# Biased maxima in two halves of the heads, first key units beside the last feed-forward chunks, gated products on GpSimd

## The reference

```
q, k, v = x Wq', x Wk', x Wv'   (32 heads of 8);   q, k = rope(q), rope(k)
gate[h, s, n] = q[h, s] . mean of k over chunk n (32 keys); later chunks out, own chunk always in; best 4 chunks chosen
p = softmax over the keys s' <= s in a chosen chunk of (q . k) / sqrt(8);   o = p v
o = o * rsqrt(mean(o^2) + 1e-6) * o_norm_weight * sigmoid(x Wg1' Wg2');   x1 = layernorm(x + o Wo')
u -> u + shared experts(u) + sum over 4 of 16 routed experts of gating * relu(u w1 + b1) w2 (+ biases);   out = layernorm(x1 + that)
```

## Time and profile before

| | us |
|---|---|
| median of 3 runs | 1453.25 (1452.52 to 1456.14) |
| the profiled execution | 1453.75 |
| its span in the trace | 1451.7 |
| maxima, one turn with feed-forward: first to last reduction | 54.3 |
| last reduction to first exponential | 10.9 |
| first to last exponential | 37.8 (38.6 and 38.7 in turns 1 and 3) |
| turn 0: the same three | 48.2, 8.9, 38.2 |
| busy share of the span | PE 92%, DVE 75%, ACT 58%, POOL 37% |

### The profile page before, as it was taken

The page is one execution under the profiler, slowest core; times in us unless marked ns, Lnnn a source line. Parts: engine busy times, 40 slices in busy tenths (PEclk is TensorE's granted clock), DMA queues, the critical chain, the costliest instruction groups (busy, mean ns, idle before and its releaser), DMA issues.

```text
span 1451.7 us, 29057 instructions
## 1 busy us (share of the span) xinstructions
PE 1332.4 (92%) x10992; PEld 738.7 (51%) x10992; DVE 1087.7 (75%) x2747; ACT 842.7 (58%) x1266; POOL 533.9 (37%) x638
## 2 busy tenths in 40 slices
PE   5677999999998999999999999989999899999597
PEld 3422475535754366534755356543665347553364
DVE  6994688957897578966889578975889668885434
ACT  5406774396735876277743967358762877439121
POOL 3203542254323642245422553235432454225143
PEclk8667999999999999999999999999999999999799
DMA  6001022200321021210222003210112102220031
GB/s 243 16 15 17 16 79 76 52 17 16 104 66 38 30 59 60 74 31 16 82 71 55 16 17 102 71 33 30 60 62 71 31 16 68 73 53 23 13 113 58
DMA packets 52283, 77.81 MB, mean 54 GB/s; under 512 B 6334, under 2 KB 26800, under 8 KB 51888
## 3 DMA queue, kind: packets, MB, share of 16 engines
q1 hardware_dynamic: 52144, 75.96, 18.0%
HBM read 67.02 MB, written 8.65 MB: 52 GB/s over the span
## 4 chain that ended last, share of the span: by engine, by line
PE 61%; DVE 19%; ACT 11%; DVEq 3%; issue 3%; DMA 2%; POOL 1%; SPq 0%; POOLq 0%
PE PS L562 14%; PE PS L574 13%; PE PS L718 8%; ACT UQ L992 7%; PE PS L492 7%; PE PS L509 3%; DVE hr L1163 3%; ACT UK L992 2%; DVE CM L1356 2%; DVEq L1155 2%; PE PS L773 2%; PE PS L413 2%; DVE CM L1275 2%; PE PS L728 2%; PE PS L483 2%
## 5 line engine op out<-in xcount | busy, mean ns | idle before, releaser
L1051 POOL TENSOR_TENSOR hp<-hr,hp 128x512 f16<-128x512 f32 (+1 forms) x200 | 237.1, 1186 | 584.1 <-ACT hp L849 520.0
L1356 DVE TENSOR_REDUCE CM<-PS 128x32 f32<-128x1024 f32 x320 | 376.2, 1218 | 23.2 <-PE PS L492 18.9
L574 PE MATMUL PS<-W,hp 128*128 128x256 f16 (+1 forms) x2400 | 323.2, 274 | 4.6 <-POOL hp L1051 3.6
L562 PE MATMUL PS<-x1T,W 128*128 128x512 f16 (+1 forms) x1200 | 320.6, 385 | 0.0
L840 ACT ACTIVATE hr<-PS,CF 128x512 f32<-128x512 f32 (+1 forms) x200 | 137.2, 686 | 234.3 <-PE PS L562 234.3
L574 PEld LDWEIGHTS PS<-W,hp 128*128 128x128 f16 (+1 forms) x2400 | 216.9, 98 | 96.1 <-issue 34.7
L849 ACT ACTIVATE hp<-hr 128x512 f16<-128x512 f32 (+1 forms) x178 | 112.5, 632 | 169.3 <-DVE hr L1163 156.2
L1163 DVE TENSOR_TENSOR hr<-hr,gB 128x512 f32<-128x512 f32 x176 | 126.2, 717 | 64.9 <-ACT hr L840 58.5
L992 ACT ACTIVATE UK<-PS 128x1024 f32<-128x1024 f32 x160 | 153.0, 1037 | 11.4 <-PE PS L509 11.0
L562 PEld LDWEIGHTS PS<-x1T,W 128*128 128x128 f16 (+1 forms) x1200 | 107.7, 100 | 100.7 <-issue 34.9
L992 ACT ACTIVATE UQ<-PS 128x1024 f32<-128x1024 f32 x160 | 150.9, 1041 | 3.1 <-PE PS L509 1.4
(11 more groups left out here) (150 smaller groups left out, 1793.8 us busy)
## 6 DMA issues: line engine op xcount, KB each, us to landing
gB<-gates SPq DMA_DIRECT2D x64, 256.0 KB, 3.3
gB<-gates SPq DMA_DIRECT2D x32, 224.0 KB, 2.9
gB<-gates SPq DMA_DIRECT2D x32, 192.0 KB, 2.9
gB<-gates SPq DMA_DIRECT2D x32, 160.0 KB, 2.6
xT<-in_xT SPq DMA_DIRECT2D x8, 512.0 KB, 5.8
qET<-rows SPq DMA_DIRECT2D x16, 256.0 KB, 5.2
v<-in_x SPq DMA_DIRECT2D x8, 512.0 KB, 4.1
gB<-gates SPq DMA_DIRECT2D x32, 128.0 KB, 2.9
```

What stands on the lines that cost most here:

```text
L562: mm = pe.matmul(PS[0:w, BK_H[c % 2], :], W1[:, a, k, bass.ds(f0, w)], x1T[:, e, k, :], start=(n == 0), stop=(n == 5))
L574: mm = pe.matmul(PS[:, BK_Y + j // 2, (j % 2) * D:(j % 2 + 1) * D], hp[0:w, slot, a, j * P:(j + 1) * P], W2[0:w, e, bass.ds(c, 1), :].rear ...
L1051: nc.gpsimd.tensor_tensor(hp[0:w, slot, 1, :], hr[0:w, slot, :], hp[0:w, slot, 0, :], ALU.subtract).then_inc(pool_hp, 1)
L1356: nc.vector.tensor_reduce(dst, src, AX.X, ALU.max).then_inc(dve_cm, 1)
```

## The change

The arithmetic stays the same. What changes is where the work stands:

- The biased maxima are made in two halves of 16 heads. The first half stands on the DVE among the reductions, after those of units 20 to 23 (`maxima(j, 0)`); the second after the last reduction. `negT` becomes [16, 2, 512], its first half copied by ACT, its second by the DVE.
- The rows of `qET` go in two sets, `s_rows[0]` for heads 0 to 15, sent while the maxima of the others go on (SP, ahead of the gates of chunk 24), and `s_rows[1]`. The first key units wait for `s_rows[0]` alone; unit 20 waits for `s_rows[1]`.
- `C_MAX` is (11, 23) in place of (11, 22) and `DEALT` has 88 parts for the 40 units in place of 77. The output gate and the transposes of the first half stand among them, in the bank that the next chunk will use.
- What is left of chunks 22 to 24 (one up, eleven down parts) and the transposes of the second half stand between the key units of groups 0 and 1.
- The gated products of chunks 11 to 22 move from the DVE to POOL, ahead of `low`. Those of 23 and 24 stay on the DVE with `split=True`, and so does the relu of chunk 24.
- The first ten key units use two pairs of banks and not three.

```diff
-PAIRS = ((0, 1, 0, 1, 0), (2, 1, 0, 2, 1), (0, 1, 2, 0, 1), (2, 0, 1, 2, 1))
-BACK = ((2, 2, 2, 2, 2), (3, 3, 3, 3, 3), (3, 2, 4, 3, 3), (3, 3, 3, 3, 2))
+PAIRS = [n % 2 if n < 2 * NU else (2, 0, 1)[(n - 2 * NU) % 3] for n in range(TU)]
+BACK = [next((k for k in range(1, n + 1) if PAIRS[n - k] == PAIRS[n]), 0) for n in range(TU)]
-C_FIRST, C_TOPK, C_MAX, C_BIAS = (0, 3), (3, 11), (11, 22), (22, 25)
+C_FIRST, C_TOPK, C_MAX, C_LATE = (0, 3), (3, 11), (11, 23), (23, 25)
-for _c in range(1, MC):
+for _c in range(1, MC + 1):
     DEALT += [(_c, 0), (_c - 2, 4), (_c, 1), (_c - 2, 5), (_c, 2), (_c - 2, 6), (_c - 1, 3)]
-DEALT += [(MC - 2, 4), (MC - 2, 5), (MC - 2, 6)]
+AT_SEL, AT_GATE, AT_NEG = (1, 2), (3, 4), 8
+HALF = H // 2
...
# SP
+                    if m < B - 1 and c == NC - 1:
+                        bias_rows(m + 1, 0)
...
# PE, among the maxima
+                        if part == 2 and cc in AT_GATE:
+                            gate_half(c, AT_GATE.index(cc))
+                        if part == 2 and cc == AT_NEG:
...
+                            maxima_rows(BK_H[(c + 1) % 2], 0)
...
# PE, key units and outputs
+                    if n < RING:
+                        pe.wait_ge(dve_cm, (b + 1) * TU + n + 1)
+                    if n == 2 * NU and m is not None:
                         pe.wait_ge(dve_z, 2 * m + 3)
+                    if n == TU // 2:
+                        pe.wait_ge(s_rows[1], 64 * (b + 1))
...
+                pe.wait_ge(s_rows[0], 64 * (b + 1))
+                unit(0, 0)
+                unit(0, 1)
+                late_up(NC - 1, (0, 1))
+                unit(0, 2)
+                late_up(NC - 1, (2,))
+                late_down(NC - 3, (1,))
+                unit(0, 3)
+                late_down(NC - 3, (2, 3))
+                unit(0, 4)
+                late_down(NC - 2, (0, 1))
+                unit(1, 0)
+                late_down(NC - 2, (2, 3))
+                unit(1, 1)
+                if m is not None:
+                    pe.wait_ge(s_hid, m * NC + NC + 1)
+                maxima_rows(BK_H[1], 1)
+                unit(1, 2)
+                if m is not None:
+                    pe.wait_ge(s_hid, (m + 1) * NC + 2)
+                outputs(0, 0, 0)
+                unit(1, 3)
+                late_down(NC - 1, (0, 1))
+                outputs(0, 0, 1)
+                unit(1, 4)
+                late_down(NC - 1, (2, 3))
+                outputs(0, 0, 2)
+                outputs(0, 0, 3)
...
# POOL
+                    for c in range(*C_MAX):
+                        gated(m, c, c % 2)
+                        low(m, c, c % 2)
+                    for c in range(*C_LATE):
                         low(m, c, c % 2)
...
# DVE, among the reductions and after them
+                        if TU // 2 <= u < TU // 2 + NT:
+                            maxima(u - TU // 2, 0)
+                if m is not None:
+                    gated(m, NC - 2, (NC - 2) % 2, split=True)
                 for j in range(NT):
...
+                    maxima(j, 1)
+                if m is not None:
+                    dve.wait_ge(pe_h, m * NC + NC)
+                    dve.wait_ge(pool_hp, m * NC + NC)
+                    s_last = (NC - 1) % 2
+                    nc.vector.tensor_scalar(hr[:, s_last, :], PS[:, BK_H[s_last], :], b1[:, NC - 1:NC], 0.0, ALU.add,
+                                            ALU.max).then_inc(s_hid, 1)
+                    dve.drain()
+                    gated(m, NC - 1, s_last, split=True)
+                dve.wait_ge(pe_neg, 2 * b + 2)
+                nc.vector.tensor_scalar(negT[:, 1, :], PS[0:HALF, BK_H[1], :], 1.0 / UNIT, None, ALU.mult).then_inc(dve_neg, 1)
```

More of the change, by code:

```diff
@@ L257, in build @@
         act_neg = sem("act_neg")
-        s_rows = sem("s_rows")
+        dve_neg = sem("dve_neg")
+        s_rows = [sem(f"s_rows{n}") for n in range(2)]
         pe_g1 = sem("pe_g1")
@@ L644, in selection_rows, with gate_half, maxima_rows @@
                     mm.then_inc(pe_sel, 1)
+                def gate_half(c, i):
+                    if m is not None:
+                        pe.wait_ge(s_hid, m * NC + c + 2)
+                    r = ROW_G1 * i
+                    for j in range(2):
+                        mm = pe.matmul(PS[:, BK_H[(c + 1) % 2], j * D:(j + 1) * D], g1T[r:r + HD, j * P:(j + 1) * P],
+                                       WG2[r:r + HD, :], start=True, stop=True, tile_position=(r, 0))
+                    mm.then_inc(pe_g, 1)
+                def maxima_rows(bank, n):
+                    pe.wait_ge(dve_bias, (2 * b + n + 1) * NT)
+                    for j in range(NT):
+                        mm = pe.transpose(PS[0:HALF, bank, j * P:(j + 1) * P], negm[:, j, HALF * n:HALF * (n + 1)], ident)
+                    mm.then_inc(pe_neg, 1)
                 if m is None:
@@ L668, in late_up, with late_down @@
+                def late_up(c, parts):
+                    for part in parts if m is not None else ():
                         up(m, c, part)
-                def late_down(c):
-                    for j in range(NT):
+                def late_down(c, parts):
+                    for j in parts if m is not None else ():
                         down(m, c, c % 2, j)
-                if m is not None:
-                    late_up(NC - 3)
-                    late_up(NC - 2)
-                    late_down(NC - 4)
@@ L942, in turn @@
                             high(m, c, (C_TOPK[0] + u) % 2)
-                for i in range(0, MAX_STEPS):
-                    for u in range(MC):
-                        c = i * MC + C_MAX[0] + u
-                        if m is not None:
-                            relu(m, c, (C_MAX[0] + u) % 2)
-                        if i == 0 and u in (1, 2):
-                            act.wait_ge(pe_sel, 2 * b + u)
-                            nc.scalar.activation(stage_sel[u - 1], PSH[:, BK_H[(c + 1) % 2], :].rearrange("p (q s) -> p q s", q=2),
-                                                 ACT.Copy, scale=-OFF).then_inc(act_sel, 1)
-                        if m is not None:
-                            high(m, c, (C_MAX[0] + u) % 2)
@@ L1132, in _ @@
         def _(dve):
[L1133 removed]
+            for credit in (dve_x1, dve_z, dve_o, dve_otok, s_gated):
                 dve.sem_inc(credit, 1)
```

197 lines of the change are left out of this document (89 added, 108 removed).

## The result

| | before | after |
|---|---|---|
| median of 4 runs, side by side | 1454.70 us (1452.52 to 1456.21) | 1520.59 us (1518.06 to 1523.06) |
| ratio | | 1.0454 (95% interval 1.0425 to 1.0483) |
| span of the profiled execution, granted clock | 1451.7 us, 0.961 | 1521.0 us, 0.941 |
| first to last reduction, turns 1 to 7 | 54.3 | 62.3 (turn 7: 65.1) |
| last reduction to first exponential | 10.8 to 11.9 | 0.3 |

The kernel became 66 us slower; 33 were forecast. The direction and the places are the forecast ones, the size is twice it. Seven turns at +9.95 us (69.6), -1.4 in turn 0 and +1.1 in all the rest are the 69.3 us by which the spans differ.

The account below looks back on a forecast made before the run. PE bounds the maxima, a DVE-to-DMA chain ends the tail, ACT's exponentials run back to back. Seven turns at +6.4 - 1.4 = +5.0 us (+35.0) and turn 0 at -1.8 give +33.2: 1453.25 + 33.2 = 1486 us, range 1450 to 1505.

Parts of the forecast that it names:

- The maxima: First to last reduction: PE's added parts, gates and transposes, with waits, lengthen it by net 6.4 us a turn.
- it falls some 2 us behind with a ring of two, which I price at 0.4 us of PE: Maxima, units 20 to 23: the DVE's new work exceeds its slack; the lag costs PE 0.4 us a turn.
- The 3.25 us of the half: DVE time for one half, 16 heads, of the biased maxima, put at 3.25 us; the whole block took 4.50.
- The upper bound of 7.5: Maxima stretch: largest growth a turn, 7.5 us, with the DVE's lag paid in full; lower bound 5.3.
- From the last unit to exponential 13: Last max unit's start to group 2's fourth exponential: 25.4 us before, 24.0 after, a gain of 1.4 a turn.
- the strict order: Behind the last max unit, masks, outputs, finish and uncovered norm follow in sequence; copy_outputs(0) ends at 22.0 us.
- The clock: Rival: idle PE at to_tokens(0) drops to 1.2 GHz; five more turns at 0.9 us, 4.5 us, 1491; chance 0.10.
- POOL's product: Gated product moved to POOL: 1.19 us each, its chain of 4.0 us hidden in a chunk's round of 4.8.
- its rival of 1520: POOL's product costs 2.37 us, so PE waits 0.4 us for each of twelve chunks: 1520; chance 0.05.
- The faster rival's point: Start kept, 1418, if copy_outputs(0) ends by 14.3 us after the last unit's start; 22 counted; chance 0.15.
- Turn 0: Turn without feed-forward: maxima +7.6 us, gap before the first exponential -9.4, together -1.8.
- the signs of being right: Maxima 60 us, start within 0.5, exponentials 47, ACT waiting some 8, copy without idle before it, PE waiting over 4.

Follow-up runs that it names:

- a_nomask: Changed kernel with the masked sum of the first half of the biased maxima left out (bias not computed there): 1508.71 us, ratio 1.0380 to the kernel before.
- a_warm: Changed kernel with 10 and 18 filler matmuls, results unused, in PE's two waits among the exponentials: 1500.73 us, ratio 1.0319 to the kernel before.
- a_copy: Changed kernel with copy_outputs(0) ahead of the layer norm in the DVE's finish, not inside it: 1502.65 us, ratio 1.0341 to the kernel before.
- a_last24: Changed kernel with chunk 24's relu, product and cast ahead of the second half's maxima, that half's transposes behind outputs (0,1): 1495.21 us, ratio 1.0292.
- a_norm3: Changed kernel with copy_outputs(0) first and the layer norm cut in three, its parts spread over the first groups: 1489.74 us, ratio 1.0254.
- a_both: Changed kernel with the first half's masked sum left out and filler matmuls in PE's two waits: 1484.27 us, ratio 1.0204 to the kernel before.
- a_spread: Changed kernel with the first half's maxima after units 20, 22, 24, 26, not 20 to 23, transposes one chunk later: 1517.16 us, ratio 1.0453.
- b_pooltail: Kernel before with the gated products of chunks 11 to 23 on POOL, those of the tail (22 and 23) included: 1456.69 us, ratio 1.0022.

## Why the prediction was wrong

- **The maxima: +6.4 forecast, +8.0 measured.** The step that failed is "it falls some 2 us behind with a ring of two, which I price at 0.4 us of PE". The 3.25 us of the half were right; their price on PE was 1.7 (62.3 to 60.6 in `a_nomask`), 1.3 more. I took most of a lag for hidden that had 1.3 to 1.8 us to hide in, at up to 0.18 us a unit. The upper bound of 7.5 had it paid in full, and even that was under 8.0. The other 0.3 us is PE's own: without the lag I had 6.3 + 0.2 - 0.5 = 6.0, and `a_nomask` has 6.3.
- **Turn 7's maxima** have 2.8 us more, in the kernel after and in `a_warm`: there PE's waits for the DVE are 0.61, 1.12 and 0.67 us, and in the 8 us from the second on (1335 to 1343) the granted clock is 0.79. `a_copy` and `a_last24` have the same three waits in turn 7 at full clock, and 1.2 us more; so about 1.2 are the waits and 1.6 the clock. In `a_norm3`, with the same program among the maxima, turn 7 is like the others. Why only this turn's waits are longer isn't shown.
- **From the last unit to exponential 13: -1.4 forecast, +0.3 in turn 6.** Every step of the strict order is within 0.4 us up to the end of the copy; lateness of the masks, the uncovered norm and the order of the queues were read rightly. Of the 1.7 us 1.6 are the three PE pieces behind the wait, all at the low clock (25.56 for 24.0); the rest is a slip in the old value, where exponential 13 began at 811.87 and not 812.04. Behind exponential 13 the same spell costs 0.8 us more (26.2 us to the end, in `a_warm` 25.4): 49.5 and not 47. In turns 1 to 4 a spell after the first wait adds up to 2 us. ACT's waits for PE came to 10.5 us, for "some 8".
- **The clock: the step that failed most.** The sum has no term for it; it was a rival with a chance of 0.10 and a price of 0.9 us a turn, 1491. The mechanism was right; the price came from the earlier trace rows, where a slow spell falls beside exponentials that set the pace themselves and hide most of it. Here the spell falls on the very pieces that ACT waits for, and there are two waits a turn. It measured 19.9 us (`a_warm`), 2.8 a turn. The Trainium skill, "TensorE: Matmul & The Clock Gate", section "What's actually happening", lets an idle TensorE fall to the lower level; by that rule all seven turns pay, and the trace agrees (0.58 in the window behind the wait of turn 6, exponentials of 49.4 us or more in every turn). Behind the shorter first wait, 2.7 us, it holds in four turns of seven. I quoted the rule and gave it a tenth.
- **Where the 36 us between forecast and trace lie:** maxima 7 x 1.6 + 2.8 = 14; exponentials and the gap ahead of them, forecast -1.4 and measured +1.5 on the mean of seven turns, 20; turn 0 (-1.4 for -1.8) and the rest 2. `a_both` takes out the first two and gives 1484.27.
- **The others.** POOL's product: 1.27 for 1.19, hidden as said; its rival of 1520 had the right time by the wrong mechanism: it needs PE to wait for the product's chain in each chunk, and in turn 6 PE has no such wait among the maxima (its one wait there that isn't for the DVE is 0.16 us, for ACT). The faster rival's point (copy ended 14.3 us after the last unit's start) was 7.7 us away, as counted. Turn 0 came near in the sum by terms that make up for each other: maxima +6.9 for +7.6, gap -9.4 as forecast, and +1.1 in the exponentials, which had no term. Of the signs of being right: start 0.3 us behind the last reduction, the copy with no idle before it, PE waiting over 4 us, all so; 60 and 47 us came out as 62.3 and 50.2.

## What to carry to other kernels

A start moved eleven microseconds ahead brings what the longest of the chains behind it allows: before moving it, write down who is late for the second and third consumer, and move those producers first (`a_last24` gave 25 us by one reordering, `a_norm3` 31, part of each from the clock). A wait of PE on the critical path of the length seen here (2.7 to 4.4 us) is priced twice, once for itself and once for the low clock that can follow it; take that price from rows where the slow work is itself on the path, not where another engine hides it. Work put on an engine that has "slack" is hidden only up to the slack of the few units that the ring spans, so divide the slack by units before calling it free.

## What the runs showed of the hardware

- Filler matmuls in two waits, 28 of them a turn, made the kernel 19.9 us faster. At the low clock (half of full, 1.2 GHz) the fp32 transposes took 1.12 for 0.65 us, outputs 1.90 for 1.04, key units 0.61 for 0.39: 1.6 to 1.8 times.
- How often the granted clock was low within 2 us of the end of a PE wait among the exponentials, in the profiled executions of the kernel after and of the eight variants of it that have such waits and no filler: behind waits of 4.1 to 4.4 us in 35 turns of 35; behind the first wait, 2.7 to 3.1 us, in 31 of 42; behind the second wait of `a_copy`, 2.5 us (once 3.4), in 3 of 7; behind waits of 1.6 to 1.9 us in 4 of 21. Below 4.1 us the same wait of the same kernel goes both ways, so its length alone doesn't decide; what does, no run here shows.
- A masked sum of 64 columns took 1.23 us where POOL's `low` of 1.16 us had begun 0.02 us ahead of it, while 128 columns took 0.29 a microsecond and a half later. 192 columns (`a_spread`) took 1.35 for 0.36, where a `low` of 1.15 us had begun 0.01 us ahead; 384 and 512 columns (`b_pooltail`) 1.14 for 0.55 and 1.31 for 0.68, with about 0.7 us of the POOL instruction left. The cost was about what was left of the POOL instruction, 0.6 to 1.0 us, and didn't go with the size of the blocked one. The reductions beside POOL's products were not touched (1222 ns against 1218).
- A GpSimd product of two fp32 tiles of 128x512 takes 1.27 us where the DVE takes 0.69.
